# Four placements changed in a two-layer attention and mixture-of-experts kernel: opening order, batch-1 key masks, the entry to the last expert stage, the last gated rows

## The chip, the cores and the metric

The kernel runs on one core of one Trainium2 chip. The core has a matrix engine (TensorE, PE in the profile), VectorE (DVE), ScalarE (ACT), GpSimd (POOL) and SyncE (SP), which issues most DMA transfers. Each engine works through its own queue in program order and waits on semaphores. The metric is device time in microseconds (us) for one execution; lower is better.

## The reference

Input `x` is 4 x 512 x 128 (2048 tokens, 16 tiles of 128), the context 4 x 77 x 128. Each of two layers is cross-attention plus a mixture of experts (8 experts, 2 chosen per token), both added to `x`:

```
x = x + _L0_xattn_ref(_layernorm(x), ctx, bias, ...)   # 16 heads of 8, q and k l2-normalised, softmax over 77 keys
x = x + _L0_ffn_ref(_layernorm(x), ...)                # silu(x W1) * (x W3) @ W2, top 2 of 8
x = x + _L1_xattn_ref(_layernorm(x), ctx, ...)         # 16 heads of 64 on one shared key/value head,
                                                       # plus silu(gate) * h @ Wff2 in parallel
x = x + _L1_ffn_ref(_layernorm(x), ...)                # gelu(x W1 + b1) @ W2 + b2, top 2 of 8
```

## The kernel before

All work is written out by hand. An attention stage is a software pipeline over 16 tiles: `step0(i)` (layer 0) and `step1(i)` (layer 1) exist once for each engine and do, in step `i`, the part for tile `t = i - const` of each operation. The order of the lines is the order of the queue. Layer 0, on the matrix engine, for one step: scores of tile `i-5` (L1642, L1645, into three PSUM banks `S`), transposes of the softmax result of tile `i-6` into `TP` (L1683 to L1707), the transposed queries of tile `i-4` (L1719, which wait for `qb`, written by VectorE), two "folded heads" (L1622), and the product with the values of tile `i-6` (L1746, "AV"). VectorE takes the maximum and subtracts it (L1016 to L1037), divides by the sum (L1101, waits for AV), writes routing rows (L1144) and, for the first steps, prepares masked keys of each batch (L962) and the layer norm statistics of four tiles at a time (L1150 to L1157, `STATS_AT`). GpSimd computes inverse roots: `rs` for four tiles (L538, `ROOTS_AT`), `qr` for one tile (L561), `rsD` (L534), and sends routing rows of tile `i-7` to DRAM by indirect DMA (L554). The first such DMA waits until SP has filled all 17,408 rows of the routing buffer with an "empty" mark (L398, 34 transfers per layer; SP issues 25 small transfers of layer 0's values, L392, before them).

The opening of layer 0 also prepares for layer 1: transposes of `Wq1` (L1605), the normalised context `cn` (L972) and its transpose, the key and value products (L1616, L1617) and the 16 folded heads, two per step by `heads_at`, in steps 7 to 14 (L1622 on PE, L694 on ACT).

After attention, `moe(l)` runs 39 jobs of 128 rows through the chosen experts, three to four stages deep: transpose (L1912), up product (L1920, or L1926 in layer 1), bias or product on VectorE (L1505, L1500), activation (L840, L835), down product (L1945). `schedule(l)` on VectorE turns the counts (L1980, the "cnt" matmul on PE) into a job table; `gates(l)` computes the gate weights and SP's wait counts (`need`). `keep_busy(n, bank)` (L1561) is `n` matmuls on ones whose result nobody reads, called "fillers" here; each shows as two matmul records. Layer 1's expert bias is transposed on PE (L1905, `b1T`) and copied by ACT (L816). In layer 1's attention the AV sum of a tile is 10 products with the values (L1873) and 4 with `wff2`, the gated rows (L1875), in one PSUM group.

## Time and profile before

| | us |
|---|---|
| three runs | 493.02, 494.76, 497.63 (median 494.76) |
| the profiled execution | 491.26, of which the span from first to last instruction is 489.3 |
| PE busy | 455.3 (93% of the span) |
| DVE busy | 366.4 (75%) |
| POOL busy | 298.1 (61%) |
| ACT busy | 233.2 (48%) |

PE's matmuls are pipelined, so its busy share is not its share of peak. The granted PE clock averages 0.969 of full over the span. In the profile the chain of work that ended last is followed back from the last instruction; it is what has to become shorter for the time to fall. An idle engine that is not on that chain costs nothing.

### The profile page before, as it was taken

The numbers are of one execution on the slowest core, as the hardware profiler recorded it, in microseconds if no ns is written. First come the engines' busy times: TensorE is split into PE (matmuls) and PEld (weight loads), VectorE is DVE, ScalarE is ACT, GpSimd is POOL, SyncE is SP. The second block draws the span as 40 slices with busy tenths as digits, with TensorE's granted clock in tenths as the row PEclk, the third lists the DMA queues.
The fourth block names the chain that finished last, engine by engine and source line by source line (L and its number), as shares of the span: only waits on it lengthen the run. The fifth ranks groups of instructions, "written<-read, shape, count | busy, mean of one in ns | idle before, by whom it ended". The sixth has DMA issues, their size and how long they took to land.

```text
span 489.3 us, 11162 instructions
## 1 busy us (share of the span) xinstructions
PE 455.3 (93%) x3313; PEld 390.3 (80%) x3313; DVE 366.4 (75%) x1232; ACT 233.2 (48%) x578; POOL 298.1 (61%) x378
## 2 busy tenths in 40 slices
PE   6569999999999799999879999999999879999996
PEld 6458888889987467676568888888889769999995
DVE  7787898989986343333488999999999867776754
ACT  3226666666654755555524343352443224554331
POOL 7535677779855347777533576776676544576661
PEclk9678999999999999999989999999999969999999
DMA  7229999920001213221461310000000122322017
GB/s 220 29 51 361 349 342 348 352 69 23 24 23 38 72 50 97 77 59 38 155 209 54 88 50 28 32 23 13 17 18 12 42 67 61 82 68 69 32 33 255
DMA packets 48972, 49.30 MB, mean 101 GB/s; under 512 B 12701, under 2 KB 34680, under 8 KB 48915
## 3 DMA queue, kind: packets, MB, share of 16 engines
q1 hardware_dynamic: 43419, 39.73, 26.5%
q0 software_dynamic: 4544, 8.44, 5.3%
q10 hardware_dynamic: 952, 0.43, 0.4%
q8 instruction: 29, 0.48, 0.4%
q14 instruction: 28, 0.23, 0.2%
HBM read 20.97 MB, written 28.35 MB: 101 GB/s over the span
## 4 chain that ended last, share of the span: by engine, by line
PE 70%; SPq 11%; DVE 5%; ACT 4%; issue 3%; POOL 3%; DMA 3%; POOLq 0%; ACTq 0%
PE ps L1945 9%; PE ps L1873 7%; PE ps L1920 7%; PE ps L1746 6%; PE ps L1926 6%; PE ps L1849 6%; SPq L392 4%; SPq L398 4%; PE ps L1825 3%; PE ps L1863 3%; PE ps L1875 3%; PE ps L1642 2%; PE ps L1956 2%; PE ps L1912 2%; POOL ys L618 2%
## 5 line engine op out<-in xcount | busy, mean ns | idle before, releaser
L618 POOL DMA_INDIRECT ys<-ysbs,backs x78 | 76.5, 980 | 62.5 <-issue 21.3
L580 POOL TENSOR_TENSOR pp<-pp,rden 128x1232 f32<-128x1232 f32 x15 | 33.7, 2249 | 33.7 <-DVE x L1312 29.1
L561 POOL TENSOR_TENSOR qr<-qsm,mhalf 128x16 f32<-128x16 f32 x16 | 47.2, 2952 | 7.2 <-DVE qsm L1002 7.1
L1500 DVE TENSOR_TENSOR big<-big,ps 128x256 f32<-128x256 f32 x39 | 16.4, 421 | 44.1 <-ACT big L835 44.1
L554 POOL DMA_INDIRECT rows<-pays,slots x32 | 33.6, 1050 | 24.2 <-DVE slots L1126 12.2
L589 POOL DMA_INDIRECT rows<-pays,slots x32 | 32.7, 1020 | 20.8 <-DVE slots L1334 10.0
L840 ACT ACTIVATE big<-big 128x512 f32<-128x512 f32 x39 | 24.6, 630 | 39.4 <-PE ps L1945 35.1
L1926 PE MATMUL ps<-xsT,wups 128*128 128x128 f32 x312 | 43.2, 284 | 0.0
L1505 DVE TENSOR_TENSOR big<-ps,b1T 128x512 f32<-128x512 f32 x39 | 27.0, 692 | 19.5 <-PE ps L1926 19.2
L1945 PE MATMUL ps<-w2b,big 128*128 (+1 forms) x312 | 41.1, 275 | 0.0
L1746 PEld LDWEIGHTS ps<-region_a,pp 128*128 128x128 f32 x320 | 37.3, 191 | 3.9 <-issue 3.3
L1746 PE MATMUL ps<-region_a,pp 128*128 128x90 f32 (+1 forms) x320 | 39.8, 280 | 0.2
L1926 PEld LDWEIGHTS ps<-xsT,wups 128*128 128x128 f32 x312 | 39.9, 200 | 0.0
L1920 PE MATMUL ps<-region_b,xsT 128*128 (+1 forms) x78 | 39.9, 594 | 0.0
L1945 PEld LDWEIGHTS ps<-w2a,big 128*128 128x128 f32 x156 | 23.2, 190 | 19.4 <-issue 14.6
L1873 PE MATMUL ps<-vals,pp 128*128 128x128 f32 x320 | 38.5, 276 | 0.0
L1945 PEld LDWEIGHTS ps<-w2b,big 128*128 128x128 f32 x312 | 37.9, 192 | 0.2 <-issue 0.2
L1873 PEld LDWEIGHTS ps<-vals,pp 128*128 128x128 f32 x320 | 37.0, 192 | 0.0
L1849 PE MATMUL ps<-keys,xT 128*128 128x462 f32 (+1 forms) x96 | 35.8, 508 | 0.0
L772 ACT COPY x2T<-ps 128x128 f32<-128x128 f32 x16 | 4.3, 267 | 59.7 <-PE ps L1764 59.7
L1849 PEld LDWEIGHTS ps<-keys,xT 128*128 128x128 f32 x96 | 17.0, 190 | 12.7 <-issue 12.7
L1642 PE MATMUL ps<-sel,biasT 128*128 128x462 bf16 (+1 forms) x96 | 26.2, 355 | 0.6 <-DVE keys L962 0.6
(319 smaller groups left out, 1254.7 us busy)
## 6 DMA issues: line engine op xcount, KB each, us to landing
rows<-empty SPq DMA_DIRECT2D x68, 258.0 KB, 4.4
xs<-rows SPq DMA_DIRECT2D x78, 64.5 KB, 1.9
region_b<-in_L_ffn_W_dram SPq DMA_DIRECT2D x2, 1024.0 KB, 9.4
yb_all<-ys SPq DMA_DIRECT2D x16, 128.0 KB, 2.4
region_a<-in_L_ffn_W_dram SPq DMA_DIRECT2D x8, 256.0 KB, 3.7
w2b<-in_L_ffn_W_dram SPq DMA_DIRECT2D x8, 256.0 KB, 4.1
keys<-ys SPq DMA_DIRECT2D x8, 256.0 KB, 3.5
ys<-ysbs,backs POOLq DMA_INDIRECT x78
```

The costliest lines, as they stand in the source:

```text
L554: pool.indirect_dma_start(rows[0][:, :], bass.IndirectOffsetOnAxis(slot[t % PB][:, k:k + 1], 0), pay[t % PB][:, k, :], None, bounds_check= ...
L561: pool.tensor_tensor(qr[s], qsm[s], mhalf[:, 0:H], ALU.pow).then_inc(a["qr"], 1)
L580: pool.tensor_tensor(p3, p3, rden[s].unsqueeze(2).to_broadcast([P, H, KEYS]), ALU.mult).then_inc(a["norm"], 1)
L589: pool.indirect_dma_start(rows[1][:, :], bass.IndirectOffsetOnAxis(slot[t % PB][:, k:k + 1], 0), pay[t % PB][:, k, :], None, bounds_check= ...
L618: pool.indirect_dma_start(ys[l][:, :], bass.IndirectOffsetOnAxis(backs[:, j % XB:j % XB + 1], 0), ysb[j % YB], None, bounds_check=2 * T - ...
L1642: mm(S[bank][:, 0:n * KEYS], biasT[0:rows_b, part, tt * P:(tt + 1) * P], sel[0:rows_b, part, :].unsqueeze(1).to_broadcast([rows_b, n, KEYS ...
L1746: ins = mm(MC[:, h * VW:e * VW], probT[s][:, c * P:(c + 1) * P], vals0[:, t // TPB, c, h:e, :].rearrange("p h v -> p (h v)"), start=c == 0 ...
L1849: ins = mm(S[bank][:, 0:n * KEYS], xT[s], keys1[:, t // TPB, h0 * KEYS:(h0 + n) * KEYS], start=True, stop=True)
L1873: mm(MC[:, 0:D], probT[s][:, c * P:(c + 1) * P], vals1[:, t // TPB, c, :], start=c == 0, stop=False)
L1920: mm(S[s][:, :], xsT[s], w13[:, expert[t], :], start=True, stop=True).then_inc(m["up"], 1)
L1926: ins = mm(S[s][:, k * P:(k + 1) * P], wup[t % WB][:, k * P:(k + 1) * P], xsT[s], start=True, stop=True)
L1945: ins = mm((MC, MD)[s][:, 0:D], hT[s][:, k * P:(k + 1) * P], w2[:, expert[t], k, :], start=k == 0, stop=k == nk - 1)
```

## The change

1. Opening of layer 0 (all engines). `cn` moves from VectorE (step 4) to ScalarE (ahead of step 3), with a small VectorE operation for its bias (`nb`). The transposes of `Wq1`, the context transpose and the second layer's key product move from steps 5 and 6 to steps 2 and 3; the value product goes to step 5. Six of the 16 folded heads are done in step 5, the others two a step in steps 6 to 10. The key transposes are split in two halves (steps 3 and 4).
2. The masked keys of batch 1 are no longer made four in a row in step 4, but two a step in steps 5 and 6, from an SBUF copy; those of batches 2 and 3 start one step later. The statistics of tile groups 2 and 3 move from steps 5 and 6 to steps 7 and 8, their roots on GpSimd from 4 and 5 to 6 and 7. The column of the router (`wc`, `centre`) moves to steps 6 and 7. The fillers ahead of step 2 become 20 instead of 8; those inside steps 3 and 4 are removed.
3. Entry to layer 1's expert stage. The bias transpose `b1T` and 8 fillers stand ahead of the last step; 4 fillers instead of 8 stand behind `cnt`. `gates(l)` runs at job 5 instead of job 2, in both layers.
4. In layer 1 the four gated rows of the last tile come ahead of its value products and of the router product of the tile before.

```
-        STATS_AT = {0: 0, 4: 1, 5: 2, 6: 3}
-        ROOTS_AT = {0: 0, 3: 1, 4: 2, 5: 3}
+        STATS_AT = {0: 0, 4: 1, 7: 2, 8: 3}
+        ROOTS_AT = {0: 0, 3: 1, 6: 2, 7: 3}
+        HEADS_FIRST = 6
         def heads_at(i):
-            return [h for h in (2 * i - 14, 2 * i - 13) if 0 <= h < H]
+            if i == 5:
+                return list(range(HEADS_FIRST))
+            return [h for h in (HEADS_FIRST + 2 * i - 12, HEADS_FIRST + 2 * i - 11) if HEADS_FIRST <= h < H]
...
+            act.wait_ge(pro["nb"], pro.count("nb", 1))
+            for b in range(NBATCH):
+                ins = act.activation(cn[:, b, :], ctx_sb[:, b, :], ACT.Identity, bias=nb[:, b:b + 1], scale=crs[:, b:b + 1])
+            ins.then_inc(pro["cn"], 1)
...
-                elif i == 4:
-                    for g in range(NG):
-                        mask_keys(1, g)
+                if i == 7:
                     centre(0)
-                    normal_context()
-                elif 6 <= i < 6 + 2 * NG:
-                    mask_keys(2 + (i - 6) // NG, (i - 6) % NG)
+                if i in (5, 6):
+                    mask_keys(1, 2 * (i - 5))
+                    mask_keys(1, 2 * (i - 5) + 1)
+                elif 7 <= i < 7 + 2 * NG:
+                    mask_keys(2 + (i - 7) // NG, (i - 7) % NG)
...
-                    if j == 2:
+                    if j == 5:
                         gates(l)
...
-            keep_busy(8, S[0])
+            keep_busy(20, S[0])
...
-                    if i == 4:
-                        keep_busy(2, S[0])
+                    if i == 5:
+                        second_values()
+                        pe.wait_ge(pro["kTs"], pro.count("kTs", NBATCH - 1))
+                        for h in heads_at(5):
+                            folded_head(h)
...
+                last = i - 6 == NT - 1
+                if last:
+                    gated_rows(NT - 1, True, False)
                 if NT - 3 <= early < NT:
                     route(1, early)
...
                     for c in range(CH):
-                        mm(MC[:, 0:D], probT[s][:, c * P:(c + 1) * P], vals1[:, t // TPB, c, :], start=c == 0, stop=False)
-                    for k in range(FF // P):
-                        ins = mm(MC[:, 0:D], gated[:, t % 4, k * P:(k + 1) * P], wff2[:, k, :], start=False, stop=k == FF // P - 1)
+                        ins = mm(MC[:, 0:D], probT[s][:, c * P:(c + 1) * P], vals1[:, t // TPB, c, :], start=c == 0 and not last, stop=last and c == CH - 1)
+                    if not last:
+                        ins = gated_rows(t, False, True)
                     ins.then_inc(a["AV"], 1)
+
+            def gated_rows(t, first, end):
+
+                pe.wait_ge(A[1]["fo"], A[1].count("fo", t + 1))
+                for k in range(FF // P):
+                    ins = mm(MC[:, 0:D], gated[:, t % 4, k * P:(k + 1) * P], wff2[:, k, :], start=first and k == 0, stop=end and k == FF // P - 1)
+                return ins
...
-                    pe.wait_ge(ld["moe1"], WEIGHTS1)
-                    tr(TP[0][:, 0:E * F1 // P], b1rows[:, :], ident[0:E * F1 // P, 0:E * F1 // P]).then_inc(pro1["b1T"], 1)
+                    pe.wait_ge(pro1["b1Ts"], pro1.count("b1Ts", 1))
...
                     if l == 0 and i == 2:
                         bias_rows()
+                        second_context()
                     if l == 0 and i == 3:
+                        second_queries()
+                        second_keys()
+                        key_rows(0, 2)
+                    if l == 0 and i == 4:
+                        key_rows(2, NBATCH)
+                    if l == 0 and i == 6:
                         pe.wait_ge(ld["o"], 48)
+                        pe.wait_ge(pro["vT1"], pro.count("vT1", 1))
                         mm(COL[0], ones_f[:, :], wr[0][:, :], start=True, stop=True).then_inc(pro["wc"], 1)
-                        key_rows()
-                    if l == 0 and i == 5:
-                        second_queries_and_context()
-                    if l == 0 and i == 6:
-                        second_keys_and_values()
+                    if l == 1 and i == NT + 6:
+                        pe.wait_ge(ld["moe1"], WEIGHTS1)
+                        tr(TP[0][:, 0:E * F1 // P], b1rows[:, :], ident[0:E * F1 // P, 0:E * F1 // P]).then_inc(pro1["b1T"], 1)
+                        keep_busy(8, TP[1])
...
-                    keep_busy(8, TP[1])
+                    keep_busy(4, TP[1])
```

Three places show what moved. Line numbers of the changed kernel are its own (L1904 is what L1875 was, L1895 what L1873 was, L1777 what L1758 was, L1582 what L1561 was, L2015 what L1980 was, L1940 what L1912 was).

First, the matrix engine at the end of layer 1's attention, from the transposed `x` of tile 14 to the first expert job. Before:

```order
L1764 MATMUL ps<-ident,x 128x128 [waits xa_a,sub_a]
L1769 MATMUL ps<-wr,x2T 128x8 [waits x2T_a]
L1873 MATMUL ps<-vals,pp 128x128 [waits PT0_a]
L1873 MATMUL ps<-vals,pp 128x128 x9
L1875 MATMUL ps<-wff,w2a 128x128 x4
L1758 MATMUL ps<-picks,upper 128x8 [waits picks_a]
...
L1758 MATMUL ps<-picks,upper 128x8 [waits picks_a]
L1759 MATMUL ps<-before,ones_b 128x8
L1980 MATMUL ps<-before,ones_b 128x8 [waits bef_a,rsel_a]
L1561 MATMUL ps<-ones_f 128x128 x8
L1905 MATMUL ps<-ident,b1rows 128x32 [waits ld_moe1]
L1912 MATMUL ps<-ident,xs 128x128 [waits xs_in0]
```

And of the change:

```order
L1783 MATMUL ps<-ident,x 128x128 [waits xa_a,sub_a]
L1904 MATMUL ps<-wff,w2a 128x128 [waits qn_a]
L1904 MATMUL ps<-wff,w2a 128x128 x3
L1788 MATMUL ps<-wr,x2T 128x8 [waits x2T_a]
L1895 MATMUL ps<-vals,pp 128x128 [waits PT0_a]
...
L2008 MATMUL ps<-ident,b1rows 128x32 [waits ld_moe1]
L1582 MATMUL ps<-ones_f 128x128 x8
L1777 MATMUL ps<-picks,upper 128x8 [waits picks_a]
L1778 MATMUL ps<-before,ones_b 128x8
L2015 MATMUL ps<-before,ones_b 128x8 [waits bef_a,rsel_a]
```

The four gated rows now stand ahead of the router product and the value products, and the bias transpose with eight fillers ahead of the last rank (L1777), which waits for `picks`, the last choice of experts.

Second, VectorE at the end of step 7 of layer 0. Before:

```order
L1101 RECIPROCAL rden<-ps 128x16 [waits AV_a]
L1120 TENSOR_TENSOR on<-ps,rden 128x128 [waits rden_a]
L1135 TENSOR_TENSOR qn<-qb,qr 128x128 [waits qr_a]
L1144 TENSOR_SCALAR pays<-x,mvD,rsD 128x2x128 [waits rsD_a]
L962 TENSOR_TENSOR keys<-wups,mask 128x308
L1002 TENSOR_SCALAR qsm<-qss 128x16 [waits qss_a]
```

And of the change:

```order
L1122 RECIPROCAL rden<-ps 128x16 [waits AV_a]
L1141 TENSOR_TENSOR on<-ps,rden 128x128 [waits rden_a]
L1156 TENSOR_TENSOR qn<-qb,qr 128x128 [waits qr_a]
L1165 TENSOR_SCALAR pays<-x,mvD,rsD 128x2x128 [waits rsD_a]
L1171 BN_STATS st<-x 128x6 [waits ld_x]
L1171 BN_STATS st<-x 128x6 x3
L1175 BN_AGGR mv<-st 128x2 [waits bnA_a]
L1175 BN_AGGR mv<-st 128x2 x3
L1178 TENSOR_SCALAR ve<-mv 128x4 [waits mvA_a]
L1183 SCALAR_TENSOR_TENSOR wr<-ps,wr 128x8 [waits wc_p]
L984 TENSOR_TENSOR keys<-wups,mask 128x308 [waits kTs_p]
```

The statistics of a group of four tiles now stand between the AV wait and the next step's work in step 7 (and in step 8).

Third, GpSimd in step 7 of layer 0, up to the first routing rows. Before:

```order
L561 TENSOR_TENSOR qr<-qsm,mhalf 128x16 [waits qsm_a]
L534 TENSOR_TENSOR rsD<-veD,mhalf 128x1 [waits veD_a]
L544 TENSOR_TENSOR x<-x,bo_bc 128x128 [waits xnA_a]
L554 DMA rows<-pays,slots 17408x129 [waits slot_a,mark_a,filled0]
L554 DMA rows<-pays,slots 17408x129
```

And of the change:

```order
L566 TENSOR_TENSOR qr<-qsm,mhalf 128x16 [waits qsm_a]
L539 TENSOR_TENSOR rsD<-veD,mhalf 128x1 [waits veD_a]
L543 TENSOR_TENSOR rs<-ve,mhalf 128x4 [waits veA_a]
L549 TENSOR_TENSOR x<-x,bo_bc 128x128 [waits xnA_a]
L559 DMA rows<-pays,slots 17408x129 [waits slot_a,mark_a,filled0]
```

The root of the fourth tile group now stands ahead of the first routing DMA.

## Rows read from the trace of the kernel before

**Rows 1.** The page, part 4: the chain's shares of the span by engine.
```profile
PE 70%; SPq 11%; DVE 5%; ACT 4%; issue 3%; POOL 3%; DMA 3%; POOLq 0%; ACTq 0%
```

**Rows 2.** The chain in order of time, 56 to 70 us: start, duration, what.
```profile
56.92 6.08 DMA rows<-empty
...
63.96 1.21 POOL rows L554
...
66.45 2.97 POOL qr L561
69.42 0.52 POOL rsD L534
```

**Rows 3.** Steps 14, 15: bounds; sum; busy PE, PEld, DVE, ACT, POOL; clock; DMA, GB/s.
```profile
100.06:107.77 7.71, 7.71 (x64) 6.56 (x62) 6.77 (x27) 5.05 (x14) 6.22 (x6) 1.00 0.09 30
107.77:114.65 6.88, 6.88 (x60) 6.29 (x58) 6.43 (x26) 4.69 (x12) 5.38 (x5) 1.00 0.07 22
```

**Rows 4.** TensorE's timeline, end of layer 1's attention to the first down product.
```profile
387.20 0.39 PE L1769 MATMUL ps<-wr,x2T 128*128 128x8 f32 x2 [0.61 <-ACT x2T L772]
389.76 1.06 PE L1875 MATMUL ps<-wff,w2a 128*128 128x128 f32 x8
394.13 0.19 PE L1758 MATMUL ps<-picks,upper 128*128 128x8 bf16 x1 [1.79 <-DVE picks L1184]
394.86 0.17 PE L1980 MATMUL ps<-before,ones_b 128*128 128x8 bf16 x1 [0.52 <-DVE before L1194]
394.89 3.76 PE L1561 MATMUL ps<-ones_f 128*128 128x128 f32 x16
405.00 1.06 PE L1945 MATMUL ps<-w2b,big 128*128 128x128 f32 x8
```

**Rows 5.** Busy time by stretch, same place; columns as in rows 3.
```profile
392.40:393.40 1.00, 0.00 (x0) 0.00 (x0) 0.92 (x7) 0.00 (x0) 0.24 (x1) 1.00 0.73 178
394.10:394.90 0.80, 0.25 (x4) 0.20 (x4) 0.77 (x7) 0.68 (x2) 0.77 (x1) 0.52 0.00 0
398.60:403.80 5.20, 4.75 (x22) 4.39 (x22) 2.17 (x8) 1.50 (x5) 0.63 (x5) 0.50 0.17 41
```

**Rows 6.** VectorE's timeline, opening: start, duration, line, operation, idle before it.
```profile
29.49 1.64 DVE L962 TENSOR_TENSOR keys<-ps,mask 128x308 fp32r<-128x308 f32 x4
31.12 1.10 DVE L972 TENSOR_SCALAR cn<-ctx_sb,cmv,crs 77x128 f32<-77x128 f32 x4
32.55 1.11 DVE L1016 TENSOR_REDUCE mx<-ps 128x12 f32<-128x924 f32 x1
45.69 0.86 DVE L1150 BATCH_NORM_STATS2 st<-x 128x6 f32<-128x128 f32 x4
67.68 0.15 DVE L1096 TENSOR_TENSOR before<-before,picks 128x8 bf16<-128x8 bf16 x1
```

**Rows 7.** TensorE's timeline: AV of tile 3, and the two heads of step 14.
```profile
66.18 2.49 PE L1746 MATMUL ps<-region_a,pp 128*128 128x144 f32 x20
104.67 0.79 PE L1622 MATMUL ps<-kT,wups 64*128 64x308 f32 x4
```

**Rows 8.** GpSimd's timeline: the root of one tile group and one bias add.
```profile
47.25 1.17 POOL L538 TENSOR_TENSOR rs<-ve,mhalf 128x4 f32<-128x4 f32 x1 [4.98 <-DVE ve L1157]
48.40 0.45 POOL L544 TENSOR_TENSOR x<-x,bo_bc 128x128 f32<-128x128 f32 x1
```

**Rows 9.** TensorE's timeline: eight fillers at full clock, and its next input.
```profile
9.24 1.95 PE L1561 MATMUL ps<-ones_f 128*128 128x128 f32 x16
14.16 0.30 PE L1660 MATMUL ps<-ident,xnA 128*128 128x128 f32 x1 [2.97 <-DVE xnA L1045]
```

**Rows 10.** VectorE's timeline: end of the job table, and the gates of layer 1.
```profile
397.97 0.16 DVE L1457 TENSOR_SCALAR sched<-rf 1x39 int32<-1x39 f32 x1
402.89 0.17 DVE L1463 TENSOR_SCALAR gtmp<-gtmp 128x16 f32<-128x16 f32 x1
403.94 0.15 DVE L1473 SCALAR_TENSOR_TENSOR need<-need_n,need_base 1x6 int32<-1x6 f32 x1
```

More of the change, by code:

```diff
@@ L856, in _ @@
                     if l == 0 and i == 4:
-                        later_keys()
-                    if l == 0 and i == 6:
-                        second_queries_and_context()
-                    if l == 0 and i == 7:
-                        second_keys_and_values()
+                        second_keys()
+                        later_keys(1)
+                    if l == 0 and i == 5:
+                        later_keys(2)
+                        later_keys(3)
                     if l == 0 and i == NT + 7:
                         fold(2, 8)
+                if l == 1:
+                    act.wait_ge(pro1["b1T"], pro1.count("b1T", 1))
+                    act.copy(b1T[:, :, :], TP[0][:, 0:E * F1 // P].rearrange("p (e k) -> p e k", e=E)).then_inc(pro1["b1Ts"], 1)
                 act.wait_ge(M[l]["margin"], M[l].count("margin", 2 - l))
@@ L966, in mask_keys, with context_shift @@
                     ins.then_inc(pro["keys0"], 1)
[L968 removed]
+            def context_shift():
                 dve.wait_ge(pro["crs"], pro.count("crs", 1))
[L971 to L973 removed]
+                dve.scalar_tensor_tensor(nb[:, :], cmv[:, :, 0], -1.0, crs[:, :], ALU.mult, ALU.mult).then_inc(pro["nb"], 1)
             def after(i):
@@ L980, in after @@
                     newton(0)
+                    context_shift()
                 elif i == 1:
@@ L1010, in step0 @@
                                       qsplit[s][:, :, 0, :, :], ALU.subtract).then_inc(a["lo"], 1)
+                if i == 4:
+                    for g in range(NG):
+                        mask_keys(0, g)
                 t = i - 5
@@ L1045, in step0 @@
                     dve.tensor_scalar(xnA[s], x[:, t, :], mv0[:, t, 0:1], rs0[:, t:t + 1], ALU.subtract, ALU.mult).then_inc(a["xnA"], 1)
-                if i == 4:
-                    for g in range(NG):
-                        mask_keys(0, g)
                 t = i - 7
@@ L1586, in bias_rows, with key_rows @@
                 ins.then_inc(pro["bT"], 1)
-            def key_rows():
+            def key_rows(b0, b1):
                 pe.wait_ge(pro["klo"], pro.count("klo", 1))
-                for b in range(NBATCH):
+                for b in range(b0, b1):
                     dst = (S[2], MC, TP[0], TP[1])[b]
```

93 lines of the change are left out of this document (42 added, 51 removed).

## The prediction

> **What bounds the kernel now.** I read the page's chain first: 70% of it lies on TensorE, but 11% on SP's queue [rows 1]. A share of SP's queue that large is a warning, so I took the chain in order of time. From 0.8 to 63 us it does not run over the opening's arithmetic at all: SP issues 25 value pieces and 34 fills without a pause, the last fill lands at 56.92 + 6.08 = 63.0, and GpSimd's first routing DMA, which waits for it, starts at 63.96 [rows 2]. Behind it, in the same queue, stand the second DMA, `qr` of tile 6 (to 69.42), and `rsD` (to 69.94), and VectorE's routing rows wait for that [rows 2]. After that the chain is TensorE with a little VectorE: step 14 of layer 0 takes 7.71 us with TensorE busy for 7.71, and step 15, without folded heads, 6.88 of 6.88 [rows 3]. Then TensorE through the expert jobs, layer 1's attention, and, at its end, a hole: TensorE waits 1.79 us for the last choice of experts, the granted clock goes from 1.00 (2.4 GHz) to about 0.5 (1.2 GHz), eight fillers take 3.76 us, and the first products of the jobs run at 0.50 until the first down product at 405.00 [rows 4, 5].
>
> **The opening.** Taken off VectorE between its first masks and the first maximum (32.55) are the four masks of batch 1 (1.64) and `cn` (1.10): 2.74 us in all [rows 6]. The first scores were ready before that maximum started, so I let the maximum come 2.7 to 3.2 us earlier. Two statistics leave steps 5 and 6, each 0.86 [rows 6] and with the two operations behind it 1.4 us; two masks a step (half of 1.64, 0.8) go in there. Six heads in a row on TensorE and ACT cost time in step 5 instead of two later. One head pair is 0.72 by the start of the next product (0.79 with its modelled end [rows 7]); three pairs with ACT's copies between them I put at 2.7 us. That falls where TensorE waited for VectorE before. AV of tile 0 then starts 2.7 us earlier, and the lead is about 3.7 after step 6. In steps 7 and 8 the two statistics, 1.4 each, come back between AV and the next queries, where nothing hides them: 3.7 - 2.8 = 0.9 us of lead at AV of tile 3 (66.18 before [rows 7]).
>
> None of this lead reaches the end. `qr` of tile 6 still ends at 69.42 because the fills still land at 63.0: SP's queue is untouched, and the values that it copies are ready before it asks for them. VectorE stops at `qn` of tile 6 until 69.42 and at the routing rows until 69.94, as before [rows 2]. So the opening is worth **0**. It can cost: the root of the fourth group (1.17) and the bias add (0.45) [rows 8] now stand ahead of the first routing DMA. The group's statistics end at about 61.4 in my walk, so GpSimd gets to its DMA at 61.4 + 1.17 + 0.45 = 63.0, level with the last fill. Bounds 0 to +0.5, and taken **+0.2**.
>
> The moved masks of batch 1 now read two SBUF tiles instead of one. In the trace a VectorE operation with two SBUF inputs takes 0.15 us at 67.68, inside the 2.97 us of GpSimd's `qr` [rows 2, 6]: no wait. The Trainium skill (SBUF — State Buffer, Who interferes with whom) says that such an operation and a GpSimd operation that reads SBUF block each other for the whole instruction. By that rule four masks could each wait up to 2.97 us behind `qr`; the trace does not show it, and the rival below carries it.
>
> **Steps 11 to 14.** The folded heads end at step 10 instead of 14. In each of the four steps TensorE was busy throughout, so a step loses the pair's 0.72 us, if VectorE (6.77 of 7.71 busy, mask included [rows 3]) can follow at 6.99. It can, barely. 4 x 0.72 = **-2.9**, taken -2.8; bounds 0 (VectorE holds the pace) and 4 x (7.71 - 6.88) = -3.3. Steps 15 on are unchanged.
>
> **The gated rows.** Four products of 0.89 us (1.06 with the modelled end) leave the place behind the values and go to a hole of 0.61 us, where TensorE waited for `x2T` [rows 4]. They overrun the hole by about 0.2: **-0.7** on the path to the last choice; bounds -0.9 and -0.4.
>
> **The entry to the last expert stage.** With that lead the last router product ends at about 391.6. The bias transpose takes 0.2 and eight fillers at full clock 1.95 [rows 9], to 393.8. The last choice is there at 394.13 - 0.7 = 393.4, so the rank is 0.4 late; VectorE asks for it only after its routing rows, which hides half: 0.2 of loss. The `cnt` matmul comes at 394.86 - 0.7 + 0.2 = 394.4 and four fillers take 1.0, to 395.4, where before the fillers ended at 394.89 + 3.76 = 398.65: 3.3 earlier [rows 4]. From there at full clock TensorE is not the bound but VectorE: its table ends 0.5 earlier than 398.13 [rows 10], at 397.6; one weight copy 0.35 and the first bias add 0.6 give 398.6; the third up product 0.9 and then the first down product, at 399.5 to 399.6 instead of 405.00 [rows 4]. Together with the gated rows this is **-5.4**, all of it carried by the following 39 jobs, which have TensorE as their bound. It needs the clock to stay up: it fell at about 394.1 after TensorE had stood idle from 392.34 [rows 4, 5], and now the fillers are in that hole. With the clock down at once, the fillers take 3.76, the last rank comes at 395.4, four more take 1.9, and the gain shrinks to about -1.2. I take -5.4.
>
> **Gates at job 5.** Six operations from 402.89 to 404.09, 1.2 us [rows 10], move to a time when VectorE idles 0.6 us a job; the up product that waits for its result has more than a job of slack. SP gets its wait counts some 3 jobs later and needs them for load 12; its loads ran ten jobs ahead. Cost 0; if that cover went, the price is the time by which load 12 misses job 12. Twenty fillers instead of eight before step 2 end at 9.24 + 2.5 x 1.95 = 14.1, and TensorE's next input came at 14.16 [rows 9]: 0.
>
> **Sum.** 0.2 - 2.8 - 5.4 = **-8.0 us**, so the profiled execution of 491.26 becomes 483.3. That execution is 3.5 below the median of the runs; the same 8.0 from 494.76 gives **486.8**.
>
> **The rivals.**
> 1. *Clock down anyway.* For it: 1.79 us of idling were enough at 392.34. Against it: that hole is filled now. Sum 0.2 - 2.8 - 1.2 = -3.8: 491.0. Chance 0.13.
> 2. *VectorE holds steps 11 to 14.* For it: 6.77 busy against 6.99 wanted, and waits of 0.2 at each hand-over. Sum 0.2 - 5.4 = -5.2: 489.6. Chance 0.10.
> 3. *The opening comes late.* GpSimd's root delays the first routing DMA by more than 0.5, or masks wait behind `qr` as in the skill's rule: four masks in two pairs, 2 x 2.97 = 5.9, of which 0.9 is lead. A typical 2 us late gives -6.2: 488.6; the whole rule gives 5.0 - 8.2 = -3.2: 491.6. Chance 0.15, of which 0.03 the rule.
> 4. *The fills do not bind.* The lead of 0.9 passes: -9.1: 485.7. Against it is the chain itself. Chance 0.08.
> 5. *Slower: TensorE stays at half clock through part of the opening.* For it: the fillers inside steps 3 and 4 are gone, TensorE may idle while six heads wait for ACT's copies, and 1.79 us of idling before 394.13 was enough for half clock [rows 4, 5]. The price: eight fillers take 3.76 at half clock [rows 4] and 1.95 at full [rows 9], a factor of 1.93, so a step of 7.7 us that is all TensorE costs up to 7.1 more. Two such steps are 14.2; less the lead of 0.9 and the other 8.2 it is +5.1: 499.9. It decides from 9.1 / 7.1 = 1.3 such steps on. Against it: VectorE sets the pace of the first steps, so a slower TensorE is partly hidden, and the opening has 2.7 us less of waiting for VectorE than before. Chance 0.04.
> 6. My forecast: chance 0.50.
>
> **How the numbers follow.** About 1% (4.9 us) is what this measurement can tell from no change. Below 489.8 lie the forecast, rivals 2 and 4 and most of 3: 0.76. Within 1%: rival 1, the rest of 3 and what the scatter of the runs (493.0 to 497.6 before) takes from the forecast: 0.20. Slower: 0.04. The range takes the forecast with its bounds and some scatter, rival 4, and reaches up through rivals 2 and 3 and to rival 1: 484.0 to 491.3.
>
> **What will show it.** The first routing DMA at 63.9 to 64.5 and `qn` of tile 6 at 69.4 to 70. Steps 11 to 14 at 7.0 us, VectorE nearly without a wait. Granted clock 1.00 from 390 through 400, and a first down product 5.4 us nearer to the end of the attention of tile 14. I am wrong if the first routing DMA starts well after 64.5, if a stretch at 0.50 shows between 391 and 400, or if the fills land earlier than 63.

## The result, and the profile after

Over twenty paired executions of each, the changed kernel has a median of 493.88 us and the kernel before 494.2. The ratio is **0.995, 95% interval 0.9928 to 0.9973**: 2.5 us faster, where I had forecast 8.0 (486.8, range 484.0 to 491.3). The direction was right, the size was not. (The ratio leaves out eight of the changed kernel's twenty executions, which took 497.3 to 502.1 us at a granted clock of 0.96 to 0.97 and of which no trace was kept; with them the medians are only 0.3 us apart.) The profiled execution of the changed kernel took 493.7 us (span 491.7, 2.4 us more than the profiled one before), so this pair of traces does not even show the gain. Reading where it went took a second pair.

The page of the changed kernel, part 4, against [rows 1]:

```profile
PE 78%; DVE 9%; ACT 4%; DMA 4%; issue 3%; SPq 1%; POOL 0%; DVEq 0%; POOLq 0%; ACTq 0%
```

SP's queue has fallen from 11% of the chain to 1%. **The opening.** VectorE's first maximum comes 3.0 us earlier than in [rows 6]; GpSimd's queue and the value products of tiles 3 and 4 answer to [rows 2, 7]. VectorE's, GpSimd's and TensorE's timelines of the changed kernel:

```profile
29.54 1.12 DVE L1040 TENSOR_REDUCE mx<-ps 128x12 f32<-128x924 f32 x1 [1.99 <-PE ps L1674]
```
```profile
62.61 1.18 POOL L543 TENSOR_TENSOR rs<-ve,mhalf 128x4 f32<-128x4 f32 x1 [3.67 <-DVE ve L1178]
63.75 0.46 POOL L549 TENSOR_TENSOR x<-x,bo_bc 128x128 f32<-128x128 f32 x1
64.39 1.21 POOL L559 DMA_INDIRECT rows<-pays,slots  x1 [0.18 <-issue]
```
```profile
66.42 2.49 PE L1765 MATMUL ps<-region_a,pp 128*128 128x144 f32 x20
...
74.85 2.38 PE L1765 MATMUL ps<-region_a,pp 128*128 128x144 f32 x19
```

The statistics end at 62.5, and their root and the bias add hold GpSimd until 64.2: the first routing DMA is 0.43 us later than before, and the value product of tile 4 (74.41 before) 0.44. The fills landed at 62.38 here. In the traces whose first routing DMA waits for them (before, stats_early, hold_stats_early) it starts 0.96 us behind the last landing, so 63.34 would have been possible; the root holds it to 64.39. From tile 4 to tile 8 the products then take 28.17 us instead of 30.98: the folded heads are gone, step after step (columns as in rows 3):

```profile
95.92:103.02 7.10, 6.96 (x59) 6.18 (x58) 6.92 (x28) 4.54 (x11) 5.90 (x6) 1.00 0.50 172
```

**The entry to layer 0's experts** was in no part of my sum. TensorE's timeline, kernel before, then the changed one:

```profile
170.15 0.30 PE L1912 MATMUL ps<-ident,xs 128*128 128x128 f32 x1 [2.11 <-ACT xsT L822]
170.28 1.02 PE L1920 MATMUL ps<-region_b,xsT 128*128 128x512 f32 x2
```
```profile
168.92 0.30 PE L1940 MATMUL ps<-ident,xs 128*128 128x128 f32 x1 [2.12 <-ACT xsT L841]
169.06 1.85 PE L1948 MATMUL ps<-region_b,xsT 128*128 128x512 f32 x2
```

The same wait of 2.1 us for ScalarE, which loads a table there (1.28 us), stands in both, but only behind the second do the products take twice as long: half clock (1.2 GHz). A second wait, earlier on this stretch, has grown as well; TensorE's timeline, before, then changed:

```profile
164.34 1.09 PE L1894 MATMUL ps<-ident,pp 128*128 128x128 f32 x8 [0.20 <-ACT pp L799]
```
```profile
163.10 1.09 PE L1923 MATMUL ps<-ident,pp 128*128 128x128 f32 x8 [1.12 <-ACT pp L821]
```

From the last value product of layer 0 to the first down product it is 22.30 us before and 24.76 after: 0.9 us of that is the longer wait, 1.5 the clock. The 2.17 us gained by then are gone.

**The entry to layer 1's experts**, against [rows 4, 5]; TensorE's timeline and the stretches of the changed kernel:

```profile
391.74 2.05 PE L1582 MATMUL ps<-ones_f 128*128 128x128 f32 x16
...
394.25 0.17 PE L2015 MATMUL ps<-before,ones_b 128*128 128x8 bf16 x1 [0.43 <-DVE rsel L1213]
394.27 1.14 PE L1582 MATMUL ps<-ones_f 128*128 128x128 f32 x8
...
400.57 0.30 PE L1940 MATMUL ps<-ident,xs 128*128 128x128 f32 x1 [1.88 <-ACT xsT L841]
400.70 1.54 PE L1954 MATMUL ps<-xsT,wups 128*128 128x128 f32 x8
402.04 1.92 PE L1973 MATMUL ps<-w2b,big 128*128 128x128 f32 x8
```
```profile
396.00:398.00 2.00, 1.66 (x14) 1.61 (x15) 1.90 (x7) 0.46 (x2) 1.70 (x2) 1.00 0.20 66
398.00:400.60 2.60, 0.72 (x8) 0.56 (x6) 1.73 (x5) 0.82 (x3) 0.71 (x5) 1.00 0.08 25
400.60:404.60 4.00, 4.00 (x22) 4.00 (x22) 1.58 (x4) 1.31 (x4) 0.00 (x0) 0.58 0.25 66
```

The fillers did hold the clock at 1.00 past 394. Then, behind a second hole, 1.88 us before the fourth row transpose, it was at half for 3.4 us. **The stream of jobs** in layer 1, 1.90 us a job before, has gaps between jobs 11 and 22 that sum to 3.9 us; the two largest, in TensorE's timeline:

```profile
430.16 1.06 PE L1973 MATMUL ps<-w2b,big 128*128 x8
431.80 0.30 PE L1940 MATMUL ps<-ident,xs 128*128 128x128 f32 x1 [0.58 <-issue]
...
432.93 1.15 PE L1973 MATMUL ps<-w2b,big 128*128 x8
435.46 0.30 PE L1940 MATMUL ps<-ident,xs 128*128 128x128 f32 x1 [1.37 <-ACT xsT L841]
```

### The profile page after: what moved, and what is told of

It is laid out like the page before. It is cut to its first block, busy times and chain, and to the rows that moved or that the text cites. A ratio compares the mean times of both kernels' runs of the same rounds, so it can differ in the third digit from the quotient of the medians.

```text
span 491.7 us, 11193 instructions
## 1 busy us (share of the span) xinstructions
PE 456.2 (93%) x3327; PEld 388.4 (79%) x3327; DVE 365.3 (74%) x1229; ACT 236.4 (48%) x583; POOL 299.1 (61%) x378
## 4 chain that ended last, share of the span: by engine, by line
PE 78%; DVE 9%; ACT 4%; DMA 4%; issue 3%; SPq 1%; POOL 0%; DVEq 0%; POOLq 0%; ACTq 0%
PE ps L1973 9%; PE ps L1765 8%; PE ps L1948 7%; PE ps L1895 7%; PE ps L1954 6%; PE ps L1868 5%; PE ps L1844 3%; PE ps L1671 3%; PE ps L1882 3%; PE ps L1904 3%; PE ps L1940 2%; PE ps L1744 2%; PE ps L1984 2%; PE ps L1674 2%; PE ps L1857 1%
## 5 line engine op out<-in xcount | busy, mean ns | idle before, releaser
L859 ACT ACTIVATE big<-big 128x512 f32<-128x512 f32 x39 | 24.7, 632 | 44.9 <-PE ps L1973 21.2
L594 POOL DMA_INDIRECT rows<-pays,slots x32 | 32.9, 1028 | 20.8 <-DVE slots L1355 10.0
L1973 PE MATMUL ps<-w2b,big 128*128 (+1 forms) x312 | 42.1, 280 | 0.0
L1948 PE MATMUL ps<-region_b,xsT 128*128 (+1 forms) x78 | 41.6, 616 | 0.0
L1954 PEld LDWEIGHTS ps<-xsT,wups 128*128 128x128 f32 x312 | 38.6, 195 | 0.1
L1895 PE MATMUL ps<-vals,pp 128*128 128x128 f32 x320 | 38.5, 276 | 0.0
L1895 PEld LDWEIGHTS ps<-vals,pp 128*128 128x128 f32 x320 | 37.0, 192 | 0.0
L1940 PE MATMUL ps<-ident,xs 128*128 128x128 f32 x78 | 21.8, 279 | 7.3 <-ACT xsT L841 6.5
```

The source lines that it names most:

```text
L594: pool.indirect_dma_start(rows[1][:, :], bass.IndirectOffsetOnAxis(slot[t % PB][:, k:k + 1], 0), pay[t % PB][:, k, :], None, bounds_check= ...
L1895: ins = mm(MC[:, 0:D], probT[s][:, c * P:(c + 1) * P], vals1[:, t // TPB, c, :], start=c == 0 and not last, stop=last and c == CH - 1)
L1948: mm(S[s][:, :], xsT[s], w13[:, expert[t], :], start=True, stop=True).then_inc(m["up"], 1)
L1954: ins = mm(S[s][:, k * P:(k + 1) * P], wup[t % WB][:, k * P:(k + 1) * P], xsT[s], start=True, stop=True)
L1973: ins = mm((MC, MD)[s][:, 0:D], hT[s][:, k * P:(k + 1) * P], w2[:, expert[t], k, :], start=k == 0, stop=k == nk - 1)
```

## The experiments

The marks below are starts in each run's own profiled execution: T4 and T15, the value products of tiles 4 and 15 in layer 0; D0, layer 0's first down product; V14, the value product of tile 14 in layer 1; D1, layer 1's second down product; the last column is the sum of the gaps over 1.90 us between jobs 1 and 35. Ratios are against the kernel before on the same chip. Chip 11 ran gates_later, entry_alone, opening_alone and gates_back; chip 15 before_again, after_again, hold_first and hold_both; chip 14 hold_later_gates, no_fillers, stats_early and hold_stats_early; chip 9 the other six. The record does not name the chip of the first two traces, before and changed kernel.

| run | T4 | T15 | T15 to D0 | V14 to D1 | gaps | span | ratio (95%) |
|---|---|---|---|---|---|---|---|
| before | 74.41 | 151.18 | 22.30 | 25.25 | 0 | 489.3 | |
| before_again | 74.41 | 151.03 | 23.60 | 25.10 | 0 | 490.2 | 1.0031 (1.0012 to 1.005) |
| gates_later | 74.12 | 151.10 | 24.72 | 24.04 | 1.6 | 491.5 | 1.0026 (0.9989 to 1.0063) |
| entry_alone | 73.98 | 150.68 | 24.65 | 23.04 | 1.9 | 491.1 | 0.9988 (0.9961 to 1.0015) |
| opening_alone | 75.53 | 149.98 | 24.69 | 23.81 | 4.8 | 493.4 | 0.9963 (0.9935 to 0.999) |
| changed kernel | 74.85 | 149.01 | 24.76 | 23.35 | 3.9 | 491.7 | 0.995 (0.9928 to 0.9973) |
| after_again | 74.99 | 149.32 | 23.81 | 20.77 | 0 | 484.8 | 0.991 (0.9875 to 0.9946) |
| after_third | 74.28 | 148.71 | 26.19 | 21.84 | 2.2 | 489.4 | 0.9979 (0.9948 to 1.0009) |
| gates_back | 75.66 | 149.99 | 24.69 | 21.93 | 2.3 | 489.5 | 0.9923 (0.9884 to 0.9962) |
| gates_back_again | 75.09 | 149.54 | 24.72 | 23.50 | 2.8 | 491.2 | 0.9914 (0.9872 to 0.9957) |
| hold_first | 74.86 | 149.18 | 22.29 | 20.93 | 0 | 481.2 | 0.9913 (0.9879 to 0.9947) |
| hold_both | 74.66 | 148.82 | 22.30 | 20.93 | 0 | 482.8 | 0.9869 (0.9813 to 0.9926) |
| hold_later_gates | 76.60 | 150.89 | 22.30 | 20.77 | 0 | 482.4 | 0.9893 (0.9837 to 0.9948) |
| no_fillers | 75.40 | 149.53 | 23.81 | 22.06 | 0 | 483.8 | 0.9917 (0.9885 to 0.995) |
| stats_early | 73.83 | 148.15 | 23.46 | 20.77 | 0 | 482.5 | 0.9918 (0.9881 to 0.9955) |
| hold_stats_early | 75.08 | 149.37 | 22.31 | 20.77 | 0 | 483.0 | 0.9895 (0.9863 to 0.9927) |
| fills_shared | 72.51 | 146.83 | 24.33 | 23.46 | 3.3 | 488.6 | 0.9826 (0.978 to 0.9873) |
| fills_shared_gates_back | 73.06 | 147.59 | 23.57 | 23.40 | 3.3 | 487.5 | 0.9813 (0.9771 to 0.9855) |
| row_first | 75.61 | 149.77 | 24.98 | 21.93 | 4.7 | 491.8 | 0.9911 (0.9877 to 0.9946) |
| all_together | 73.36 | 147.64 | 23.63 | 21.40 | 2.9 | 484.8 | 0.9844 (0.9809 to 0.9879) |

### Which part cost what

**gates_back**, on the changed kernel:

```
-                    if j == 5:
+                    if j == 2:
                         gates(l)
```

> The changed kernel with gates(l) back at job 2 in both layers, all else as changed. Theory G (the later gates cause the stream's holes): SP waits for the wait counts of gates before load 12 and then loads six of them into registers, so every load from job 12 on was about 2.5 us later, and TensorE had 3.9 us of holes between the down products of jobs 11 and 22. With gates at job 2 the holes are gone: down products 1.90 apart from job 1 to 35, median about 3 to 4 us below the changed kernel's, near 488. Theory H (the holes are an accident of that one execution or come from GpSimd's 3.9 us pause, which both kernels have): the time is that of the changed kernel within 1 us, and a hole can show here too.

**gates_later** is the same edit the other way, alone on the kernel before.

> The kernel before with gates(l) moved from job 2 to job 5 and nothing else. Theory G: load 12 of layer 1 is issued 3 to 4 us later than 409.2, and the run shows holes in the stream of down products between jobs 12 and 22 of 2 to 4 us in all: 496 to 498. Theory H: no holes beyond those before; the time stays within 1 us of the kernel before (494).

Gaps of 1.6 us (gates_later) and 2.3 us (gates_back) stand in the two, so theory G's 3.9 us are not what the gates cost: with the gates at job 2 the stream is still broken, most of it (1.7 us) at job 16.

**entry_alone** and **opening_alone** do one part each on the kernel before. The edit of entry_alone (ScalarE's copy of the bias moves ahead of its jobs with it):

```
+                    if l == 1 and i == NT + 6:
+                        pe.wait_ge(ld["moe1"], WEIGHTS1)
+                        tr(TP[0][:, 0:E * F1 // P], b1rows[:, :], ...).then_inc(pro1["b1T"], 1)
+                        keep_busy(8, TP[1])
...
-                    keep_busy(8, TP[1])
+                    keep_busy(4, TP[1])
```

> The kernel before with only the entry to layer 1's experts changed: bias transpose and eight fillers ahead of the last rank, four fillers behind the count instead of eight; gated rows and gates unmoved. Theory E (the entry keeps the clock up through the table, then loses it in a second hole of 1.7 us, where the fourth row transpose waits for ScalarE): full clock to about 401, half clock for 3 to 4 us instead of 10; second down product 1.0 to 1.5 us earlier than 406.90, 492.5 to 493.5. My forecast's theory (clock stays up throughout): first down product 4.7 us earlier, 489.5. Rival (the clock falls at 394 as before): no gain, 494.

> The kernel before with only the opening, the heads and the key masks of layer 0 changed. Theory F (the 2.2 us gained by the end of layer 0's attention are lost at the entry to its experts, because TensorE's clock falls to half there during the 2.1 us wait for ScalarE's table load): steps 11 to 14 at 7.05 us, last value product near 149.0, half clock from 169 to 173, first down product of layer 0 at 173.5 to 173.8, time 494 as before. Rival (the clock stays up there in this version): first down product at 171.3 to 172.4, time 492 to 493.

entry_alone gains 2.2 us from V14 to D1 on the trace of before, but only 1.0 on gates_later, which has before's entry on the same chip; its time moves by 0.1%, inside the interval. The clock stayed at 1.00, also in the hole before the fourth row transpose, where theory E had it fall. Even so the first down product is only 2.4 us nearer to V14 than on the trace of before, and 1.2 nearer than in gates_later, not the 4.7 us of my forecast's theory. opening_alone ends layer 0's attention 0.7 to 1.1 us earlier than those two, its entry to the experts at half clock (0.50 from 171 to 172), 0.4% less time: theory F's marks, without a gain to give back beyond 1 us, since the versions with the old opening enter at half clock on this chip as well.

### Was the trace of before typical?

**before_again** and **after_again** are the two kernels unchanged.

> The kernel before, unchanged, for a second profiled execution. Theory B (the profiled execution on which I predicted was not a typical one): layer 0's experts are entered at half clock here (first down product near 175.5 instead of 173.5), the entry to layer 1's experts loses less to half clock than 5 us of the clock's share, and the stream of layer 1 has a hole of 1.6 us or more at job 16. Rival (the execution was typical): marks within 0.5 us of 173.5, 387.5, 405.0 and 473.1.

> The changed kernel, unchanged, for a second profiled execution. If gates at job 5 cause several holes (theory G), holes of 3 to 4 us in all stand between jobs 11 and 22 again, more than the single one of 1.6 us at job 16 that the other versions have. If they were an accident (theory H), one hole at job 16 remains. Layer 0's experts at half clock at their entry again: first down product 173.7 to 174.8.

TensorE's timeline of before_again at the entry to layer 0's experts:

```profile
169.99 0.45 PE L1912 MATMUL ps<-ident,xs 128*128 128x128 f32 x1 [2.11 <-ACT xsT L822]
170.23 1.92 PE L1920 MATMUL ps<-region_b,xsT 128*128 128x512 f32 x2
```

Half clock behind the same 2.11 us, in the kernel before. Of four profiled executions with the old opening, three enter at half clock (23.6 to 24.7 us from T15 to D0); the one I predicted on was the exception. No gaps in either run: theory G falls, since after_again has gates at job 5 and a stream without a hole. On this chip the pair differs by 1.7 us at T15, 1.5 at D0, 5.9 at D1 and 5.4 in span.

The traces fall into two sorts, and the first pair has one of each. In the ten of chips 9 and 11, TensorE waits 1.1 to 1.5 us for ScalarE ahead of the transposes in the stretch from T15 to D0, and layer 1's stream has gaps. In the eight of chips 14 and 15 that wait is 0.2 us and there are no gaps. The first trace of the kernel before has the second sort's marks (0.20, no gaps), that of the changed kernel the first sort's (1.12, gaps). So their difference is not the change alone.

A wait at a third place shows how much the clock varies between executions. In layer 1's opening TensorE waits 2.33 to 2.34 us for VectorE in all twenty traces. Behind it the clock stands at 0.50 for a time in fifteen, and D0 to V14 takes 207.7 to 208.2 us; in five (hold_first, hold_later_gates, no_fillers, fills_shared_gates_back, all_together) it does not, and the same stretch takes 206.4. Nothing in my sum or in the experiments touches that place.

### The clock at the two entries

**hold_first** adds, to gates_back; **hold_later_gates** to the changed kernel:

```
                         tr(MA[:, 0:P], xs[j % XB][:, 0:D], ident[:, :]).then_inc(m["Tx"], 1)
+                        if l == 0 and j == 0:
+                            keep_busy(8, S[1])
```

> The changed kernel with gates at job 2 and, new, eight fillers on TensorE behind the first row transpose of layer 0's experts, where it waits 2.1 us for ScalarE's table load. Theory F (clock falls because of that wait): no half clock from 169 to 173, first down product of layer 0 at 172.4 to 173.0 instead of 174.7, time 1.7 us below the same kernel without them: 489.8. Rival (the clock falls later in another hole of the same length): no gain.

> The changed kernel, gates at job 5 as changed, with one addition: eight fillers on TensorE behind the first row transpose of layer 0's experts. It isolates the half clock at that entry: no half clock near 169, from the last value product of layer 0 to the first down product 22.3 us instead of 23.8 to 24.8, and 1.5 us less time than the changed kernel. Rival: the gain of hold_first came from its gates at job 2, and this one has none.

**hold_both** adds to hold_first `if l == 1 and j == 3: keep_busy(6, TP[1])` ahead of the fourth row transpose's wait.

> As hold_first, and six more fillers ahead of the fourth row transpose of layer 1's experts, where TensorE waits 1.3 to 1.9 us for ScalarE. Where the clock fell in that hole (the profiled execution of the changed kernel), 1.7 us are saved; where it did not (gates back at job 2), nothing: 488.5 to 490. Rival: the fillers overrun the hole by 0.2 us and cost that.

Busy time by stretch, after_again, then hold_later_gates:

```profile
170.00:172.00 2.00, 2.00 (x5) 0.79 (x4) 0.42 (x1) 0.54 (x2) 0.00 (x0) 0.55 0.00 0
```
```profile
168.00:170.00 2.00, 1.67 (x16) 1.51 (x15) 0.00 (x0) 1.68 (x4) 0.00 (x0) 1.00 0.26 63
170.00:172.00 2.00, 2.00 (x7) 0.68 (x6) 0.42 (x1) 0.81 (x3) 0.00 (x0) 1.00 0.01 3
```

With fillers in that wait the clock stays at 1.00 and T15 to D0 is 22.29 to 22.31 in the four runs of chips 14 and 15 that have them (hold_first, hold_both, hold_later_gates, hold_stats_early), against 23.8 in after_again: 1.5 us, as theory F had it. The three fills_shared versions on chip 9 have the fillers too and need 23.6 to 24.3; the wait of 1.5 us that chip 9 adds ahead of the transposes makes up 1.3 of it. The times do not show the gain: beside after_again on the same chip hold_first has the same ratio (0.9913 and 0.991), and the interval of hold_later_gates (0.9893) overlaps with both. It is shown in the marks alone. hold_both's extra fillers met a clock that was up anyway.

**no_fillers** leaves `keep_busy(8, TP[1])` out ahead of the last rank.

> The changed kernel without the eight fillers ahead of the last rank in layer 1 (bias transpose stays there; four fillers behind the count stay). If they hold the clock (my forecast's mechanism): half clock from about 393 for 3 to 10 us as before, second down product 1.7 to 3.5 us later. Rival (the earlier bias transpose and the smaller number of fillers are what helps): no half clock, second down product within 0.5 us of the changed kernel's, counted from the value product of tile 14.

Its timeline and stretches have the old fall back, smaller:

```profile
391.29 0.18 PE L1777 MATMUL ps<-picks,upper 128*128 128x8 bf16 x1 [1.61 <-DVE picks L1205]
```
```profile
392.00:398.00 6.00, 5.54 (x25) 5.10 (x26) 4.17 (x17) 1.78 (x5) 3.50 (x8) 0.50 0.15 47
```

D1 comes 1.3 us later than in after_again. So the fillers work as forecast, but what they avert in this one trace is 1.3 us, below the 1.7 to 3.5 that I expected and far from the whole of [rows 5]; the rest of the gain at this entry comes with the other three edits there, which no run separates.

### The fills of the routing buffer

**stats_early** puts `STATS_AT` and `ROOTS_AT` back to the values before; **hold_stats_early** does it together with hold_later_gates' edit.

> The changed kernel with the statistics of tile groups 2 and 3 back in steps 5 and 6 and their roots back in steps 4 and 5; all else as changed. In the changed kernel the third group's statistics on VectorE (to 62.5), its root and the bias add on GpSimd stand ahead of the first routing DMA, which starts at 64.39 instead of 63.96. Theory S (that root costs the 0.4 to 0.6 us, and the fills bind behind it): first value product 1 to 3 us later than 40.9, first routing DMA at 63.5 to 64.0, value product of tile 4 at 74.0 to 74.4 instead of 74.85, time 0.5 us less than the changed kernel. Rival 4 of the prediction (the fills do not bind): value product of tile 4 at 73.5 or earlier. Other rival (the shift comes from the masks, not from the root): tile 4 stays at 74.85 to 75.0.

> stats_early and hold_later_gates together, the candidate for the best version: 0.5 and 1.5 us below the changed kernel, so 2 us in all if both theories hold. Where stats_early gives nothing it equals hold_later_gates.

GpSimd's and TensorE's timelines of hold_stats_early:

```profile
64.34 1.21 POOL L559 DMA_INDIRECT rows<-pays,slots  x1 [6.26 <-DMA rows<-empty]
```
```profile
63.64 2.49 PE L1765 MATMUL ps<-region_a,pp 128*128 128x144 f32 x20
...
75.08 2.49 PE L1765 MATMUL ps<-region_a,pp 128*128 128x144 f32 x20
```

Tile 3 is 2.8 us earlier than in the changed kernel, GpSimd is idle for 6.26 us until the last fill is in, and tile 4 comes at 75.08: the whole lead is swallowed at the place that I had named. In stats_early, which is the same kernel up to there, the fills ended earlier (62.43 instead of 63.38; a line of its chain), and tile 4 came at 73.83:

```profile
56.41 6.02 DMA rows<-empty
```

So theory S's 0.5 us lie inside the scatter of the fills, and hold_stats_early's ratio is that of hold_later_gates (0.9895 and 0.9893), not 0.5 us better. **fills_shared** moves that bound: on hold_stats_early, ScalarE issues six of the 34 fills where it idles.

```
+            for n in range(ACT_FILLS):
+                act.dma_start(dst0[n], empty[:, :, :].rearrange("p r c -> p (r c)")).then_inc(filled[0], 16)
...
-                for n in range(SLOTS // P // 4):
+                for n in range(0 if l else ACT_FILLS, SLOTS // P // 4):
```

> hold_stats_early with six of layer 0's 34 fills issued by ScalarE at 10.5 us, where it idles, instead of by SP from 34 us. If the fills bind the first routing DMA (my step): last fill lands near 57.5 instead of 62.4, first routing DMA starts at 59 to 62 instead of 63.4 to 64.3, value product of tile 4 at 71.0 to 73.0 instead of 73.8 to 75.1, and the time is 1.5 to 3 us below hold_stats_early. Rival (the indirect DMA is slow for another reason, or GpSimd's root and q rescaling bind): value product of tile 4 within 0.5 us of hold_stats_early's, no change of time.

> As fills_shared, with gates(l) back at job 2. Theory G (gates at job 5 delay the loads and cost holes): 1 to 4 us below fills_shared. Theory H (no effect): equal within 1 us. Theory K (at job 2 they stand in VectorE's way while the pipeline fills): 0.2 to 1.2 us above fills_shared, from the last value product to the second down product of layer 1.

Timelines of fills_shared:

```profile
61.37 1.35 POOL L560 DMA_INDIRECT rows<-pays,slots  x1 [2.18 <-issue]
```
```profile
72.51 2.49 PE L1769 MATMUL ps<-region_a,pp 128*128 128x144 f32 x20
```

In the three versions with shared fills (fills_shared, fills_shared_gates_back, all_together) the fills land at 57.9 to 59.9, the first routing DMA starts at 61.4 to 61.9 instead of 63.4 and 64.3, and tile 4 comes at 72.5 to 73.4 instead of 73.8 and 75.1, 0.5 to 2.6 us earlier: the fills were the bound. They are so no longer: the DMA now starts 1.5 to 4.0 us behind the last landing, not 0.96. Ratios 0.9826 and 0.9813 are the best of the study, but they come from chip 9 and those without shared fills from chip 14; T15, 0.5 to 2.5 us earlier than in stats_early and hold_stats_early, accounts for a part of them only.

### The gates once more, and ScalarE's order

after_third and gates_back_again are the changed kernel and gates_back again, side by side on one chip.

> The changed kernel unchanged, beside gates_back_again on one chip. From its two profiled executions: 3 to 4.5 us below the kernel before, one half clock at the entry to layer 0's experts.

> The changed kernel with gates at job 2, beside after_third. Theory G: 1 to 4 us below after_third. Theory H: equal within 1 us. Theory K: 0.2 to 1.2 us above it.

After_third's 1.0 us below the kernel before misses the 3 to 4.5 expected. The gates at job 5 lose in this pair (0.9979 against 0.9914, the intervals just overlapping), and are equal in fills_shared's pair. The traces show no cost: after_third's span is the shorter by 1.8 us, and where the clock stayed up, V14 to D1 is 20.77 with the gates at job 5 (after_again, hold_later_gates, stats_early, hold_stats_early) and 20.93 with the gates at job 2 (hold_first, hold_both). That is 0.16 us in favour of job 5, theory K's sign and just below its size. Whether the times hide a cost of up to 3 us stays open. **row_first** lets ScalarE copy the third transposed row ahead of the first activation in layer 1; **all_together** is fills_shared with it.

> The changed kernel; on ScalarE in layer 1 the copy of the third transposed row now stands ahead of the first activation instead of behind it. Theory A (that order is what my sum left out): TensorE's fourth row transpose comes about 1.2 us earlier, the wait ahead of it falls from 1.3 to 1.9 us to below 0.5, and the first down product is 0.8 to 1.3 us nearer to the last value product than in the changed kernel; time 1 us less. Rival (VectorE's bias add, not the copy, sets the first down product): the transpose comes earlier but the first down product moves by less than 0.3 us.

> fills_shared with gates at job 5 and row_first's order: value product of tile 4 near 72.5, no half clock at the entry of layer 0's experts or one earlier, first down product of layer 1 at 12 us behind the last value product; 1 us below fills_shared, some 9 us below the kernel before if the parts add. Rival: the parts overlap, and it equals fills_shared.

In row_first the wait ahead of the fourth transpose is gone, but the clock had fallen before it (0.50 at 399 and 400), and V14 to the first down product is 20.04 us, as in its neighbours (19.9 to 20.8). all_together, with the clock up throughout, has 19.51 against 19.95 in after_third: 0.4 of the 0.8 to 1.3 expected. But that measure takes in 0.5 us by which its first bias add ended later behind V14. VectorE's and TensorE's timelines of all_together:

```profile
395.32 0.69 DVE L1531 TENSOR_TENSOR big<-ps,b1T 128x512 f32<-128x512 f32 x1 [0.91 <-PE ps L1961]
```
```profile
397.13 1.06 PE L1980 MATMUL ps<-w2b,big 128*128 128x128 f32 x8
```

From the end of that bias add the first down product follows after 1.12 us, against 2.05 in after_again and after_third, which have the old order and full clock there. So the order is worth 0.9 us, as theory A had it. The ratio, 0.9844, is that of fills_shared: in the time nothing of it shows.

## Why the prediction was wrong, step by step

1. **The base.** I took one profiled execution for the kernel and its median for the same thing. That execution entered layer 0's experts without half clock, as one of the four with that opening did, and lost the most of the four at layer 1's entry: 25.25 us from V14 to D1, where the others with that entry needed 25.10 (before_again), 24.04 and 23.81. A gain priced from its hole at layer 1 was priced from the deepest of four.
2. **The entry to layer 1, -5.4: the step that failed, mis-sized.** After_again shows what it is worth undisturbed: V14 to D1 20.77 us, 4.3 to 4.5 less than the two traces of before. Its parts up to the bias add held: the gated rows brought the last transposed `x` 0.9 us nearer to V14 (0.7 forecast; the products' 0.89 less the hole's 0.61 is an overrun of 0.3, not 0.2, and TensorE did not pay even that), the table ended 15.9 us behind V14 (forecast 15.95), and VectorE's first bias add at 16.8 (16.95). But I let the first down product follow the third up product at once. ScalarE's timeline of after_again shows what stands between:

```profile
398.02 0.63 ACT L859 ACTIVATE big<-big 128x512 f32<-128x512 f32 x1 [2.11 <-DVE big L1526]
398.56 0.25 ACT L841 COPY xsT<-ps 128x128 f32<-128x128 f32 x1
```

   The copy that the fourth transpose needs waits behind an activation; the transpose and the up product follow, and the first down product comes at 400.04, 1.0 us behind my sum; all_together, with the copy first, has 0.9 of that back. The profiled execution of the changed kernel gained 1.9 us instead of 4.5, and lost the other 2.6 in two ways. Its first bias add came late, with the table in time and the clock still at 1.00; VectorE's timeline, changed kernel, then after_again:

```profile
398.91 0.69 DVE L1526 TENSOR_TENSOR big<-ps,b1T 128x512 f32<-128x512 f32 x1 [0.87 <-PE ps L1954]
```
```profile
397.32 0.67 DVE L1526 TENSOR_TENSOR big<-ps,b1T 128x512 f32<-128x512 f32 x1
```

   It ends 17.8 us behind V14 instead of 16.8. The seven traces with the whole new entry on chips 9 and 11 have 17.8 to 18.4, the six on chips 14 and 15 with the fillers 16.8; what delays TensorE there is open. Then the clock fell in the hole before the fourth transpose, which is my rival 1 in another place: 1.6 us. On the chips with the gaps, executions with the old entry show 23.8 and 24.0 us, the eight with the new one 21.4 to 23.5, a mean of 22.6: 1.4 us.
3. **The opening, +0.2: right in kind, too small.** The fills swallow the lead; hold_stats_early and fills_shared show it. In the changed kernel itself two ends compete at the first routing DMA: the last fill and the root, which I had level at 63.0. The statistics end at 62.5 instead of my 61.4, so the root binds in nine of the eleven traces with this opening, by 0.1 to 2.7 us, 1.05 in the first. The fills, which I took as fixed, land anywhere from 62.2 to 64.2. T4 was 0.4 to 0.6 us late in the first two traces of the changed kernel, and 1.4 to 1.7 on chip 11, the one that ran both openings (75.5 and 75.7 against 74.0 and 74.1); there the fills themselves landed at 63.7 and 64.2 instead of 62.2 and 62.6. Over these eleven T4 averages 75.2 (74.3 to 76.6), over the four with the old opening 74.2: +1.0, beyond my bound of +0.5. In four of the eleven the DMA starts at 65.08 or later, which I had named as a sign of being wrong: that is the first half of my rival 3.

   The masks of batch 1 never met GpSimd's `qr` in the changed kernel: in its VectorE timeline they stand at 35.69 and 44.09, 0.86 us a pair, and `qr` begins at 36.72 and 45.11. They did meet another GpSimd operation that reads SBUF, the root `rs`. VectorE's and GpSimd's timelines of stats_early:

```profile
37.32 0.86 DVE L984 TENSOR_TENSOR keys<-ysbs,mask 128x308 fp32r<-128x308 f32 x2
37.49 1.17 POOL L543 TENSOR_TENSOR rs<-ve,mhalf 128x4 f32<-128x4 f32 x1 [6.15 <-DVE ve L1178]
```

   In 46 cases over the twenty traces a mask with two SBUF inputs overlaps an `rs`. Each such mask takes 0.47 us, as the others do, and in stats_early the second of the pair starts and ends inside `rs`. The Trainium skill's rule (SBUF — State Buffer, Who interferes with whom) would have one of the two block the other for its whole length. Here neither does, and the measurement decides for these two operations; a mask beside `qr` occurs in no run here.
4. **Steps 11 to 14, -2.8: right.** 28.17 and 28.19 us instead of 30.98 and 30.83. VectorE follows, busy for 6.92 of 7.10. But the stretch behind it, T15 to D0, stood in my sum at nothing without a reason, and cost the first trace 2.5 us: 1.5 of half clock, which three of the four traces with the old opening have too, and 0.9 of the wait that goes with the chip.
5. **Gates, 0: open**, as above.
6. **The stream, 0.** The gaps (up to 4.8 us, most of them at jobs 11 to 22) go with the chip, not with the version: they are in all ten runs on two chips, in none of eight on two others, and versions with either entry and either place of the gates are on both sides. What makes them is not settled. GpSimd's pause of 3 to 4 us ahead of a scatter stands in both kernels' traces, also where there is no gap.

The first pair of spans adds up like this: -2.2 to T15, +2.5 to D0, -0.1 to V14, -1.9 to D1, +3.9 of gaps, +0.2 behind the stream: +2.4. The second pair: -1.7, +0.2, 0, -4.3, 0, +0.4: -5.4.

As averages: -0.9 (T15, chip 11) and -1.4 (entry) make -2.3 on the chips with gaps, near the -2.5 of the ratio of 0.995; -1.7 and -4.3 make -6.0 on chip 15, where the medians differ by 4.4. On neither is it 8.0.

## What to carry to other kernels

Take more than one profiled execution before pricing a hole in which the clock fell: whether a wait of 2 us costs half clock changed between executions of the same kernel. Before comparing two traces, see whether a stretch that the change does not touch agrees in both. A lead is worth nothing ahead of a queue of transfers that ends when it ends; move the transfers first (six fills on another queue gave 0.5 to 2.6 us where the reordered opening gave none). And where a pipeline fills, write out every engine's queue up to the first result, since one copy behind an activation cost 0.9 us.

## What the runs showed of the hardware

TensorE's granted clock dropped to 0.50 at a wait of 2.1 us at the entry to layer 0's experts in 12 of the 13 profiled executions without fillers there, and in none of the seven with them (one of which had dropped and recovered before). Behind the wait of 2.33 us in layer 1's opening, which has no fillers, it stood at 0.50 in 15 of 20. In 46 cases a VectorE product with two SBUF inputs ran at the same time as a GpSimd root that reads SBUF: the product took 0.47 us as without one, the root 1.16 to 1.26 us, where those without a product beside them took 1.01 to 1.19. The identical kernel, run as before_again, came out at 1.0031 with an interval of 1.0012 to 1.005: differences of 0.3% say nothing here. On four chips the kernel before had medians of 490.45, 491.15, 494.77 and 496.33 us, and 497.39 on the last of them at another time.
